# GpSimd takes the cosine products of the rotary embedding, VectorE copies both heads' transposed probabilities

## The chip, the cores and the metric

The kernel runs on one core of one Trainium2 chip. The metric is the device time of one execution in microseconds. A core has a matrix engine (TensorE, PE in the rows; its weight loads are PEld), a vector engine (VectorE, DVE), an activation engine (ScalarE, ACT), a general engine (GpSimd, POOL) and DMA queues; each engine runs its own list of instructions in order, and they meet only at semaphores. Matrix products land in PSUM, everything else lies in SBUF.

## The reference

Two transformer layers over 8 sequences of 128 tokens with 128 channels, in fp32. Layer 0 has a self-attention and a cross-attention (16 heads of 64 channels each) and an MLP; queries and keys are turned by a rotary embedding. Layer 1 has the same three parts with heads of 8 channels. Cut to what matters here (layer 0):

```python
def _rope(x, sin, cos):                 # on q and on k
    xe, xo = x[..., ::2], x[..., 1::2]
    re = xe * cos - xo * sin
    ro = xe * sin + xo * cos
    return jnp.stack((re, ro), axis=-1).reshape(x.shape)

def _attn(xq, ctx, wq, wkv, wo, bo):
    q = _heads(xq @ wq)
    k, v = jnp.split(ctx @ wkv, 2, axis=-1)
    q, k, v = _rope(q, sq, cq), _rope(_heads(k), sk, ck), _heads(v)
    sim = jnp.einsum('bhnd,bhmd->bhnm', q, k) * DH ** (-0.5)
    a = jax.nn.softmax(sim, axis=-1)
    return merge(jnp.einsum('bhnm,bhmd->bhnd', a, v)) @ wo + bo

x = _attn(adaln(x), adaln(x), ...) + x
x = _attn(adaln(x), ln(context), ...) + x
x = gelu(adaln2(x) @ w1 + b1) @ w2 + b2 + x
```

## The kernel before

Layer 0's attention is cut into 32 items (`ITEMS`): self- or cross-attention, times two halves of the batch (four sequences each), times eight pairs of heads. An item's tiles are 128 x 512 fp32: 128 channels of a pair of heads, by four sequences of 128 tokens. The work is a software pipeline written out by hand: each engine has a function `l0_slot(s)`, called for s = -2 to 31, and in slot s it handles stages of several items. There is no planner; the order within each engine's slot is the order of its code.

The stages of an item m, and who does them:

- `fill(m, f)` on PE: the query projection (f = 0) into PSUM bank X, the key projection (f = 1) into bank Y, the values (f = 2) into bank T[1]. In slot s these are for item s + 2.
- `evacuate_raw(m, f)` on ACT copies X or Y into the SBUF tile `raw` (for item s + 2); `evacuate_v` copies the values.
- `swap(m)`, two DMAs for each f on SP's queue, writes `raw` with neighbouring channels exchanged into `swp`.
- `rope_sine(m, f)` on GpSimd multiplies `swp` by the sines in place (item s + 1, L241). It waits first for the scores of slot s (`scores[0]`).
- `rope_cosine(m, f)` on VectorE multiplies the projection, read from the PSUM bank, by the cosines into `qk` (L652): for the keys of item s + 1, and the queries of item s + 2.
- `rope_sum(m, f)` on VectorE adds `swp` to `qk` (item s + 1, L658).
- `score(s)` on PE, `row_max(s, hh)` on VectorE (L635, from PSUM), `exp0(s, hh)` on ACT (L374), `normalise(s, hh)` on VectorE (a small reciprocal, then L642: both operands, `prob` and `rz`, lie in SBUF), for each of two heads hh.
- `transpose_probs(s, hh)` on PE (L908) into PSUM banks T[0] and T[1]; the copies to `probT` are VectorE's for head 0 (L648) and ACT's for head 1 (L380), in slot s + 1; then `prob_values` and `project_out` on PE.

PE's slot in order: score(s), transposes of (s-1, head 1), fill(s+2, 0), project_out(s-2), background, fill(s+2, 2), fill(s+2, 1), transposes of (s, head 0), prob_values(s-1). "Background" is the work of layer norms, context projections (slots 7 to 12), residuals and the MLP, set into single slots. A fill into X or Y waits until the bank has been read: by `rope_cosine`, which itself waits for `evacuate_raw`. In slot 26 GpSimd also computes a layer norm's inverse deviations, `inv_std(0, 2)` (L223), which VectorE's `ln_normalise` (L581) in the same slot waits for. Layer 1 begins behind slot 31, with `l1_slot(0)` taking the last probabilities of layer 0.

Of the kernel before, what the change touches and what calls it, by code (L numbers as in the profile page):

```python
# [58 lines left out]
def build(nc, small_in, x_in, ctx_in, ctxT_in, wqkv_in, wo_in, wmod_in, wsq_in, wff_in, row_in, out):  # L59
    es = ExitStack()  # L60
    with es:
# [157 lines left out]
        @block.gpsimd  # L219
        def _(pool):  # L220
            def inv_std(half, k):
                pool.wait_ge(ln_mv[half], k + 1)
                nc.gpsimd.tensor_tensor(rstd[:, half, :], vare[:, half, :], neg_half[:, 0:HALF], ALU.pow).then_inc(  # L223
                    ln_rstd[half], 1)

            def normalise_first(half, k):

                pool.wait_ge(ln_rstd[half], k + 1)
                for u in range(2):
                    last = nc.gpsimd.tensor_scalar(xn[:, HALF * half + u, :], x[:, HALF * half + u, :], mv[:, half, u, 0:1],  # L230
                                                   rstd[:, half, u:u + 1], ALU.subtract, ALU.mult)
                last.then_inc(ln_xn[half], 1)

            def context_inv_std(half):
                pool.wait_ge(ctx_mv, half + 1)
                nc.gpsimd.tensor_tensor(rstd_c[:, batches(half)], vare_c[:, batches(half)], neg_half[:, 0:HALF],
                                        ALU.pow).then_inc(ctx_rstd, 1)

            def rope_sine(m, f):
                pool.wait_ge(swapped[f][m % 2], 32 * (m // 2 + 1))  # L240
                nc.gpsimd.tensor_tensor(four(swp[:, m % 2, f, :]), four(swp[:, m % 2, f, :]), sin[f], ALU.mult).then_inc(  # L241
                    rope_sin[f], 1)

            def split_rows():
                pool.wait_ge(ld_rows, 16)
                src, done = rows, 0
                for j in range(3):
                    nc.gpsimd.tensor_copy(parts[:, j, :], src[:, :]).then_inc(row_part, 1)
                    done += 1
                    pool.wait_ge(row_part, done)  # L250
                    if j < 2:
                        nc.gpsimd.tensor_tensor(rest[:, :], src[:, :], parts[:, j, :], ALU.subtract).then_inc(row_part, 1)
                        done += 1
                        pool.wait_ge(row_part, done)
                        src = rest

            def mask_keys(a, half, j):

                pool.wait_ge(proj_out, AT["ck" if a else "k", half] + 1)
                if a:  # L260
                    for hh in range(2):
                        pool.wait_ge(scores1[hh], RUN * half + 2 * j + 2)
                ins = nc.gpsimd.tensor_scalar(km[:, half, j, :], k1[:, a, half, :], small[:, MASK + j:MASK + j + 1], None,
                                              ALU.mult)
                ins.then_inc(km_rest[half] if j else km_first[half], 1)

            def stage_values(half):
                pool.wait_ge(pv1, RUN * half + RUN)
                src = cv[:, half, :].rearrange("p (n h d) -> p n h d", h=2, d=DH1)
                for hh in range(2):  # L270
                    ins = nc.gpsimd.tensor_copy(value_slots(half, hh), src[:, :, hh, :])
                ins.then_inc(vst_out[half], 1)

            def l0_slot(s):
                if s in (2, 4):
                    context_inv_std(s // 2 - 1)
                if s in (12, 20):
                    inv_std(s // RUN - 1, 1)
                if 0 <= s < ITEMS - 1:
                    pool.wait_ge(scores[0], s + 1)  # L280
                if s + 1 < ITEMS:
                    rope_sine(s + 1, 0)
                    rope_sine(s + 1, 1)
                if s in (26, 30):
                    inv_std(0, 2 if s == 26 else 3)

            pool.dma_start(rows[:, :], row_in).then_inc(ld_rows, 16)
            inv_std(0, 0)
            inv_std(1, 0)
            split_rows()  # L290
            pool.memset(vst[:, :, :], 0.0).then_inc(padded, 1)
            pool.wait_ge(padded, 1)
            lanes = vst[:, :, :].rearrange("p a (n w) -> p (a n) w", w=2 * VW)
            pool.memset(lanes[:, :, DH1:DH1 + 49:48], 1.0).then_inc(padded, 1)
            pool.wait_ge(ld_tab, 16)
            for s in range(-1, ITEMS):
                l0_slot(s)
            for j in range(1, SLOTS):
                mask_keys(0, 0, j)
            inv_std(1, 2)  # L300
            normalise_first(1, 2)
            inv_std(1, 3)
            normalise_first(1, 3)
            for j in range(1, SLOTS):
                mask_keys(0, 1, j)
            for half in range(2):
                for j in range(SLOTS):
                    mask_keys(1, half, j)
                stage_values(half)
                inv_std(half, 4)  # L310
                normalise_first(half, 4)
            for half in range(2):
                inv_std(half, 5)
                normalise_first(half, 5)

        @block.scalar
        def _(act):
# [43 lines left out]
            def evacuate_raw(m, f):  # L361
                act.wait_ge(filled[f], m + 1)
                if m >= 2:
                    act.wait_ge(swapped[f][m % 2], 32 * (m // 2))
                nc.scalar.activation(raw[:, m % 2, f, :], (X, Y)[f][:, :], ACT.Copy).then_inc(raw_out[f], 1)  # L365

            def evacuate_v(m):
# [2 lines left out]

            def exp0(s, hh):
                act.wait_ge(rowmax[hh], s + 1)
                for u in range(HALF):
                    last = nc.scalar.activation(prob[:, hh, bcols(u)], S[hh][:, bcols(u)], ACT.Exp,  # L374
                                                bias=nmax[:, s % 2, hh, u:u + 1], accum_out=zsum[:, s % 2, hh, u:u + 1])
                last.then_inc(exps[hh], 1)

            def copy_T0(s):
                act.wait_ge(probs_T[1], s + 1)
                nc.scalar.activation(probT[:, s % 2, 1, :], T[1][:, :], ACT.Copy).then_inc(copied[1], 1)  # L380

            def evacuate_o(s):
                act.wait_ge(pv, s + 1)
# [39 lines left out]
            def l0_slot(s):  # L423
                loads(s)
                if s >= 2:
                    evacuate_o(s - 2)
                if s >= 1:
                    copy_T0(s - 1)
                if s >= 0:
                    exp0(s, 0)  # L430
                if s + 2 < ITEMS:
# [55 lines left out]
            def l1_slot(s):  # L487
                if s == 0:
                    evacuate_o(ITEMS - 2)
                    copy_T0(ITEMS - 1)  # L490
                if s == RUN:
                    copy_T1(s - 1)
                    evacuate_proj("q", 1)
# [56 lines left out]
        def _(dve):  # L550
# [92 lines left out]
                                        rz[:, s % 2, hh, :].unsqueeze(2).broadcast_to([P, HALF, P]), ALU.mult).then_inc(  # L643
                    norms[hh], 1)

            def copy_T0(s):
                dve.wait_ge(probs_T[0], s + 1)
                nc.vector.tensor_copy(probT[:, s % 2, 0, :], T[0][:, :]).then_inc(copied[0], 1)  # L648

            def rope_cosine(m, f):  # L650
                dve.wait_ge(raw_out[f], m + 1)
                nc.vector.tensor_tensor(four(qk[:, m % 2, f, :]), four((X, Y)[f][:, :]), cos[f], ALU.mult).then_inc(  # L652
                    rope_cos[f], 1)

            def rope_sum(m, f):
                dve.wait_ge(rope_sin[f], m + 1)
# [4 lines left out]
            def l0_slot(s):  # L661
                if s >= 1:
                    normalise(s - 1, 1)
                if s >= 0:
                    row_max(s, 0)
                    row_max(s, 1)
                if 0 <= s + 1 < ITEMS:
                    rope_cosine(s + 1, 1)
                if s in (26, 30):
                    ln_aggregate(2 if s == 26 else 3, 0)  # L670
                if s >= 1:
                    copy_T0(s - 1)
                if 0 <= s + 1 < ITEMS:
                    rope_sum(s + 1, 0)
                if s >= 0:
                    normalise(s, 0)
                if 0 <= s + 1 < ITEMS:
                    rope_sum(s + 1, 1)
                if s + 2 < ITEMS:
                    rope_cosine(s + 2, 0)  # L680
                background0(s)

            def background0(s):
# [57 lines left out]
            def l1_slot(s):  # L741
# [8 lines left out]
                    row_max1(s, 0)  # L750
                    row_max1(s, 1)
                if s == 0:
                    copy_T0(ITEMS - 1)
                middle1(s)
                if 1 <= s <= ITEMS and not first:
                    copy_T1(s - 1)
# [51 lines left out]
            ln_stats(0, 1)  # L808
            ln_aggregate(0, 1)
            dve.wait_ge(ld_tab, 16)  # L810
            l0_slot(-2)
            silu_condition()
            nc.vector.tensor_scalar(bq_scaled[:, :], vcol("b_q"), DH1 ** -0.5, None, ALU.mult)
            ln_normalise(0, 1)
# [7 lines left out]
        def _(pe):  # L822
# [33 lines left out]
            def fill(m, f):  # L856
# [8 lines left out]
                weights = wqkv[:, a * RUN + n, :]  # L865
                if f == 0:
                    if m:
                        pe.wait_ge(rope_cos[0], m)
                    if m == 31:
                        pe.wait_ge(gelu_done, 3)  # L870
                    mm(X[:, :], weights[:, 0:P], hT[:, half, :], True, True).then_inc(filled[0], 1)
                elif f == 1:
                    if m:
                        pe.wait_ge(rope_cos[1], m)
                    mm(Y[:, :], weights[0:width, P:2 * P], kv[:, half, :], True, True).then_inc(filled[1], 1)
                else:
                    if m:
# [120 lines left out]
            def l0_slot(s):  # L998
# [14 lines left out]
                    fill(s + 2, 1)  # L1013
                if s == 31:
                    project("q", 0)
                    pe.wait_ge(rope_cos[1], ITEMS)
                    project("k", 0)
                    project_values(0)
                transpose_probs(s, 0)
# [2 lines left out]
                if s == 28:  # L1022
# [1 line left out]
                    up(0, 0, 0, S[0])  # L1024
                    pe.wait_ge(exps[1], 29)
                    up(0, 0, 1, S[1])
                    pe.wait_ge(rope_cos[0], 31)
                    up(0, 0, 2, X)
                    pe.wait_ge(gelu_done, 1)
                    up(0, 0, 3, S[0])  # L1030
                if s == 30:
                    pe.wait_ge(rope_cos[0], ITEMS)
                    transpose_norm(3, 0, [X, X])

            def background0(s):
# [254 lines left out]
```

## Time and profile before

| what | value |
|---|---|
| median of three runs | 438.99 us (434.75 to 439.44) |
| the profiled execution | 439.93 us |
| its span | 437.9 us |
| TensorE clock granted in it, mean | 0.969 of full speed |
| PE / DVE / ACT / POOL busy | 89% / 73% / 70% / 31% |
| layer 0, first to last score | 22.28 to 267.26 us |

The span is the stretch from the first to the last instruction in the profile; the execution's time has 2.03 us more around it. Busy shares are averages over both layers; the argument needs single slots.

### The profile page before, as it was taken

To read this page: it belongs to the slowest core of one execution; us is meant where nothing else is said; L and a number is where in the kernel's file an instruction comes from. 1 tells how busy PE (TensorE), PEld (TensorE's weight loads), DVE (VectorE), ACT (ScalarE), POOL (GpSimd) and SP (SyncE) were. 2 spreads that over 40 slices of the span, in tenths; PEclk is the share of its full clock that TensorE was granted. 3 is DMA by queue.
4 is the path that set the end of the run, shared out by engine and by line. 5 is a ranking of instruction groups with operands and counts; after the bars stand their busy time and mean duration, and the time that the engine had idled before them with its cause. 6 is when DMAs were issued, how large, how long until landed. Compare 5 with 4: busy or idle time off the path is not lost.

```text
span 437.9 us, 9911 instructions
## 1 busy us (share of the span) xinstructions
PE 391.6 (89%) x3600; PEld 292.8 (67%) x3600; DVE 318.4 (73%) x685; ACT 307.1 (70%) x1052; POOL 136.6 (31%) x120
## 2 busy tenths in 40 slices
PE   7678999999989999989988988989898898898976
PEld 3355677777768777667666566867576687687654
DVE  4799898988878899978997575664557557557430
ACT  2277687877877786777768856697698678668722
POOL 1834433324333334324253230420473402002020
PEclk9899999999999999999999998999999979869999
DMA  5434424232441212121211010000000000000000
GB/s 171 149 111 126 162 91 157 72 121 77 132 159 48 99 71 75 57 77 61 85 61 62 36 49 1 2 2 0 1 1 2 1 1 2 1 2 1 1 24 24
DMA packets 17075, 26.08 MB, mean 60 GB/s; under 512 B 3615, under 2 KB 7973, under 8 KB 16901
## 3 DMA queue, kind: packets, MB, share of 16 engines
q1 hardware_dynamic: 13572, 18.43, 11.9%
q10 hardware_dynamic: 3424, 7.03, 5.3%
q8 instruction: 29, 0.48, 0.5%
q14 instruction: 18, 0.14, 0.1%
q0 software_dynamic: 32, 0.00, 0.0%
HBM read 8.15 MB, written 0.52 MB: 20 GB/s over the span
## 4 chain that ended last, share of the span: by engine, by line
PE 57%; DVE 23%; ACT 8%; issue 6%; POOL 2%; DMA 1%; POOLq 0%; SPq 0%; DVEq 0%; ACTq 0%
PE bank L824 44%; PE bank L1084 6%; PE bank L908 5%; DVE qk L658 4%; ACT prob L374 3%; DVE qk L652 3%; DVE nmax L720 3%; DVE prob L642 3%; DVE nmax L635 3%; DVE probT L648 2%; DVE xn L581 2%; ACT raw L467 1%; ACT hT L357 1%; PE bank L835 1%; DMA swp<-raw 1%
## 5 line engine op out<-in xcount | busy, mean ns | idle before, releaser
L241 POOL TENSOR_TENSOR swp<-swp,small 128x512 f32<-128x512 f32 x64 | 82.9, 1305 | 142.8 <-PE bank L824 115.4
L374 ACT ACTIVATE prob<-bank,nmax 128x128 f32<-128x128 f32 x256 | 91.2, 389 | 1.3 <-DVE nmax L635 1.3
L467 ACT ACTIVATE raw<-bank,nmax 128x128 f32<-128x128 f32 x256 | 73.4, 386 | 22.8 <-DVE nmax L720 22.8
L635 DVE TENSOR_REDUCE nmax<-bank 128x4 f32<-128x512 f32 x64 | 41.2, 685 | 29.1 <-PE bank L824 28.8
L720 DVE TENSOR_REDUCE nmax<-bank 128x4 f32<-128x512 f32 x64 | 41.2, 685 | 28.6 <-PE bank L824 28.5
L374 ACT ACTIVATION_READ_ACCUMULATOR prob<-bank,nmax 128x1 f32 x256 | 59.1, 231 | 0.0
L658 DVE TENSOR_TENSOR qk<-qk,swp 128x512 f32<-128x512 f32 x64 | 51.3, 803 | 5.0 <-POOL swp L241 5.0
L824 PE MATMUL bank<-hT,wqkv 128*128 128x512 f32 x96 | 49.8, 603 | 5.1 <-DVE qk L652 4.1
L908 PEld LDWEIGHTS bank<-small,prob 128*128 128x128 f32 x256 | 27.8, 140 | 39.0 <-DVE prob L642 29.0
L908 PE MATMUL bank<-small,prob 128*128 128x128 f32 x256 | 41.3, 284 | 13.6 <-DVE prob L642 13.3
L642 DVE TENSOR_TENSOR prob<-prob,rz 128x512 f32<-128x512 f32 x64 | 50.1, 782 | 2.2
L824 PE MATMUL bank<-km,q 32*128 32x128 f32 x512 | 39.6, 295 | 10.7 <-ACT raw L467 6.0
L223 POOL TENSOR_TENSOR rstd<-vare,neg_half 128x4 f32<-128x4 f32 x12 | 12.3, 1023 | 113.9 <-DVE vare L573 113.8
L652 DVE TENSOR_TENSOR qk<-bank,small 128x512 f32<-128x512 f32 x64 | 46.3, 723 | 0.7 <-ACT raw L365 0.7
L824 PEld LDWEIGHTS bank<-km,q 32*128 32x128 f32 x512 | 33.4, 197 | 18.0 <-issue 8.0
L380 ACT ACTIVATE probT<-bank 128x512 f32<-128x512 f32 x32 | 19.1, 597 | 37.2 <-PE bank L908 37.1
L365 ACT ACTIVATE raw<-bank 128x512 f32<-128x512 f32 x64 | 40.6, 636 | 1.9 <-PE bank L824 1.8
L824 PEld LDWEIGHTS bank<-wo,oT 128*128 128x128 f32 x256 | 33.0, 191 | 12.7 <-issue 12.1
L824 PE MATMUL bank<-probT,v 128*64 128x128 f32 x512 | 35.8, 283 | 4.0 <-ACT hT L357 3.2
L824 PE MATMUL bank<-qk 64*128 64x128 f32 x512 | 37.5, 286 | 2.0 <-DVE qk L658 1.0
L1084 PE MATMUL bank<-small,raw 128*128 128x128 f32 x256 | 38.4, 297 | 0.1
L824 PEld LDWEIGHTS bank<-qk 64*128 64x128 f32 x512 | 31.5, 189 | 8.4 <-issue 7.7
(106 smaller groups left out, 631.8 us busy)
## 6 DMA issues: line engine op xcount, KB each, us to landing
swp<-raw SPq DMA_DIRECT2D x128, 128.0 KB, 2.0
wqkv<-in_wqkv ACTq DMA_DIRECT2D x15, 192.0 KB, 2.5
wo<-in_wo ACTq DMA_DIRECT2D x2, 512.0 KB, 4.0
wff<-in_wff ACTq DMA_DIRECT2D x1, 1024.0 KB, 5.7
wsq<-in_wsq ACTq DMA_DIRECT2D x1, 576.0 KB, 4.6
x<-in_x SPq DMA_DIRECT2D x2, 256.0 KB, 4.2
wmod<-in_wmod ACTq DMA_DIRECT2D x1, 512.0 KB, 5.1
out_x<-x SPq DMA_DIRECT2D x2, 256.0 KB, 2.3
```

Of the source, the lines that this page charges most:

```text
L241: nc.gpsimd.tensor_tensor(four(swp[:, m % 2, f, :]), four(swp[:, m % 2, f, :]), sin[f], ALU.mult).then_inc(rope_sin[f], 1)
L365: nc.scalar.activation(raw[:, m % 2, f, :], (X, Y)[f][:, :], ACT.Copy).then_inc(raw_out[f], 1)
L374: last = nc.scalar.activation(prob[:, hh, bcols(u)], S[hh][:, bcols(u)], ACT.Exp, bias=nmax[:, s % 2, hh, u:u + 1], accum_out=zsum[:, s % ...
L467: last = nc.scalar.activation(prob1[:, s % 2, hh, bcols(u)], SB[(2 * s + hh) % 3][:, bcols(u)], ACT.Exp, bias=nmax[:, s % 2, hh, u:u + 1])
L635: nc.vector.tensor_reduce(nmax[:, s % 2, hh, :], four(S[hh][:, :]), AX.X, ALU.max, negate=True).then_inc(rowmax[hh], 1)
L642: nc.vector.tensor_tensor(four(prob[:, hh, :]), four(prob[:, hh, :]), rz[:, s % 2, hh, :].unsqueeze(2).broadcast_to([P, HALF, P]), ALU.mul ...
L652: nc.vector.tensor_tensor(four(qk[:, m % 2, f, :]), four((X, Y)[f][:, :]), cos[f], ALU.mult).then_inc(rope_cos[f], 1)
L658: nc.vector.tensor_tensor(qk[:, m % 2, f, :], qk[:, m % 2, f, :], swp[:, m % 2, f, :], ALU.add).then_inc(roped[f], 1)
L720: nc.vector.tensor_reduce(nmax[:, s % 2, hh, :], four(SB[(2 * s + hh) % 3][:, :]), AX.X, ALU.max, negate=True).then_inc(rowmax1[hh], 1)
L824: return nc.tensor.matmul(o, lhsT, rhs, start=start, stop=stop, skip_group_check=True)
L908: last = nc.tensor.transpose(T[hh][:, bcols(u)], prob[:, hh, bcols(u)], ident)
L1084: last = nc.tensor.transpose(T[hh][:, bcols(u)], prob1[:, s % 2, hh, bcols(u)], ident)
```

## The change

GpSimd takes over both cosine products of every item. It reads them from the SBUF copy `raw`, not from the PSUM banks. They stand last in its slot: after the two sines of item s + 1 come the two cosines of item s + 2. Its slot now waits for both heads' scores. The banks X and Y are free once `evacuate_raw` is done, so PE's fills wait for `raw_out` in place of `rope_cos`. VectorE loses its cosines, and gets the copy of head 1's transposed probabilities, ahead of head 0's; its two sums move together behind `normalise(s, 0)`. ACT loses that copy; its exponentials now wait for the transposes of the item before.

```diff
@@ gpsimd
+            def rope_cosine(m, f):
+                pool.wait_ge(raw_out[f], m + 1)
+                nc.gpsimd.tensor_tensor(four(qk[:, m % 2, f, :]), four(raw[:, m % 2, f, :]), cos[f], ALU.mult).then_inc(
+                    rope_cos[f], 1)
@@ gpsimd l0_slot(s), now from s = -2
                 if 0 <= s < ITEMS - 1:
                     pool.wait_ge(scores[0], s + 1)
-                if s + 1 < ITEMS:
+                    pool.wait_ge(scores[1], s + 1)
+                if 0 <= s + 1 < ITEMS:
                     rope_sine(s + 1, 0)
                     rope_sine(s + 1, 1)
+                if s + 2 < ITEMS:
+                    rope_cosine(s + 2, 0)
+                    rope_cosine(s + 2, 1)
                 if s in (26, 30):
                     inv_std(0, 2 if s == 26 else 3)
@@ scalar: evacuate_raw(m, f), m >= 2
                     act.wait_ge(swapped[f][m % 2], 32 * (m // 2))
+                    act.wait_ge(rope_cos[f], m - 1)
@@ scalar: exp0(s, hh)
+                if s:
+                    act.wait_ge(probs_T[hh], s)
@@ scalar: copy_T0 and its calls in l0_slot and l1_slot(0) are gone
@@ vector: rope_cosine and its calls are gone
-            def copy_T0(s):
+            def copy_T0(s, hh):
@@ vector l0_slot(s)
                     row_max(s, 0)
                     row_max(s, 1)
-                if 0 <= s + 1 < ITEMS:
-                    rope_cosine(s + 1, 1)
                 if s in (26, 30):
                     ln_aggregate(2 if s == 26 else 3, 0)
                 if s >= 1:
-                    copy_T0(s - 1)
-                if 0 <= s + 1 < ITEMS:
-                    rope_sum(s + 1, 0)
+                    copy_T0(s - 1, 1)
+                    copy_T0(s - 1, 0)
                 if s >= 0:
                     normalise(s, 0)
-                if 0 <= s + 1 < ITEMS:
+                if s + 1 < ITEMS:
+                    rope_sum(s + 1, 0)
                     rope_sum(s + 1, 1)
-                if s + 2 < ITEMS:
-                    rope_cosine(s + 2, 0)
@@ vector l1_slot(0)
-                    copy_T0(ITEMS - 1)
+                    copy_T0(ITEMS - 1, 0)
+                    copy_T0(ITEMS - 1, 1)
@@ tensor: fills of X and Y, and the other users of these banks
-                        pe.wait_ge(rope_cos[0], m)
+                        pe.wait_ge(raw_out[0], m)
```

## Rows read from the trace of the kernel before

**Rows 1.** The page: busy times, and the chain that ended last by engine.

```profile
PE 391.6 (89%) x3600; PEld 292.8 (67%) x3600; DVE 318.4 (73%) x685; ACT 307.1 (70%) x1052; POOL 136.6 (31%) x120
PE 57%; DVE 23%; ACT 8%; issue 6%; POOL 2%; DMA 1%; POOLq 0%; SPq 0%; DVEq 0%; ACTq 0%
```

**Rows 2.** Timeline of PE, scores of single slots: start, us, what.

```profile
137.40 1.16 PE L824 MATMUL bank<-qk 64*128 64x128 f32 x16
...
157.86 1.16 PE L824 MATMUL bank<-qk 64*128 64x128 f32 x16
165.05 1.16 PE L824 MATMUL bank<-qk 64*128 64x128 f32 x16
172.51 1.16 PE L824 MATMUL bank<-qk 64*128 64x128 f32 x16
```

**Rows 3.** Groups of 100 to 200 us, by form: busy us, mean ns | idle before.

```profile
L241 POOL TENSOR_TENSOR swp<-swp,small 128x512 f32<-128x512 f32 x27 | 34.1, 1275 | 58.1 <-PE bank L824 45.9 <-DMA swp<-raw 11.9
L658 DVE TENSOR_TENSOR qk<-qk,swp 128x512 f32<-128x512 f32 x27 | 20.3, 750 | 1.2 <-POOL swp L241 1.2
L652 DVE TENSOR_TENSOR qk<-bank,small 128x512 f32<-128x512 f32 x27 | 18.4, 681 | 0.0
L648 DVE COPY probT<-bank 128x512 f32<-128x512 f32 x14 | 9.5, 679 | 0.0
L380 ACT ACTIVATE probT<-bank 128x512 f32<-128x512 f32 x13 | 7.8, 597 | 14.6 <-PE bank L908 14.6
```

**Rows 4.** Timeline of slot 17, from the end of its scores.

```profile
152.16 1.29 DVE L635 TENSOR_REDUCE nmax<-bank 128x4 f32<-128x512 f32 x2 [0.84 <-PE bank L824]
152.21 2.62 POOL L241 TENSOR_TENSOR swp<-swp,small 128x512 f32<-128x512 f32 x2 [4.27 <-PE bank L824]
...
154.62 0.62 ACT L365 ACTIVATE raw<-bank 128x512 f32<-128x512 f32 x1
...
155.50 0.69 DVE L642 TENSOR_TENSOR prob<-prob,rz 128x512 f32<-128x512 f32 x1
...
156.94 0.67 ACT L365 ACTIVATE raw<-bank 128x512 f32<-128x512 f32 x1
```

**Rows 5.** Timelines of DVE and POOL where they overlap, slots 9 and 26.

```profile
93.12 0.68 DVE L658 TENSOR_TENSOR qk<-qk,swp 128x512 f32<-128x512 f32 x1
93.25 1.68 POOL L241 TENSOR_TENSOR swp<-swp,small 128x512 f32<-128x512 f32 x1 [1.22 <-DMA swp<-raw]
...
218.77 2.94 POOL L241 TENSOR_TENSOR swp<-swp,small 128x512 f32<-128x512 f32 x2 [4.27 <-PE bank L824]
218.81 1.76 DVE L642 TENSOR_TENSOR prob<-prob,rz 128x512 f32<-128x512 f32 x1
```

**Rows 6.** Timelines of POOL and PE, start of layer 0.

```profile
14.73 3.51 POOL L291 MEMSET vst<- 128x4096 f32 x1
...
18.49 2.49 POOL L241 TENSOR_TENSOR swp<-swp,small 128x512 f32<-128x512 f32 x2
...
22.28 1.16 PE L824 MATMUL bank<-qk 64*128 64x128 f32 x16 [0.51 <-DVE qk L658]
...
36.84 1.16 PE L824 MATMUL bank<-qk 64*128 64x128 f32 x16
```

**Rows 7.** The waits of layer 0, 22 to 275 us: total, times, longest.

```profile
POOL swp L241 <- DMA swp<-raw: 27.1, 16, 5.4
```

**Rows 8.** Timeline of slot 26: inverse deviations and the normalisation that waits for them.

```profile
222.94 1.01 POOL L223 TENSOR_TENSOR rstd<-vare,neg_half 128x4 f32<-128x4 f32 x1 [1.24 <-DVE vare L573]
...
225.99 1.11 DVE L581 TENSOR_SCALAR xn<-x,mv,rstd 128x128 f32<-128x128 f32 x4
```

**Rows 9.** Timeline of slot 0 of layer 1.

```profile
277.16 0.68 DVE L648 COPY probT<-bank 128x512 f32<-128x512 f32 x1
...
277.89 1.09 PE L824 MATMUL bank<-probT,v 128*64 128x128 f32 x16 [0.46 <-DVE probT L648]
```

**Rows 10.** The chain that ended last, in slot 13: start, us, what.

```profile
122.53 0.05 ACT probT L380
```

More of the change, by code:

```diff
@@ L295, in _ @@
             pool.wait_ge(ld_tab, 16)
-            for s in range(-1, ITEMS):
+            for s in range(-2, ITEMS):
                 l0_slot(s)
@@ L376, in exp0 @@
                 last.then_inc(exps[hh], 1)
-            def copy_T0(s):
-                act.wait_ge(probs_T[1], s + 1)
-                nc.scalar.activation(probT[:, s % 2, 1, :], T[1][:, :], ACT.Copy).then_inc(copied[1], 1)
             def evacuate_o(s):
@@ L426, in l0_slot @@
                     evacuate_o(s - 2)
-                if s >= 1:
-                    copy_T0(s - 1)
                 if s >= 0:
@@ L644, in normalise @@
                     norms[hh], 1)
[L646 to L653, printed above, removed]
+            def copy_T0(s, hh):
+                dve.wait_ge(probs_T[hh], s + 1)
+                nc.vector.tensor_copy(probT[:, s % 2, hh, :], T[hh][:, :]).then_inc(copied[hh], 1)
             def rope_sum(m, f):
@@ L671, in l0_slot @@
                 if s >= 1:
-                    copy_T0(s - 1)
-                if 0 <= s + 1 < ITEMS:
-                    rope_sum(s + 1, 0)
+                    copy_T0(s - 1, 1)
+                    copy_T0(s - 1, 0)
                 if s >= 0:
                     normalise(s, 0)
-                if 0 <= s + 1 < ITEMS:
+                if s + 1 < ITEMS:
+                    rope_sum(s + 1, 0)
                     rope_sum(s + 1, 1)
-                if s + 2 < ITEMS:
-                    rope_cosine(s + 2, 0)
                 background0(s)
@@ L752, in l1_slot @@
                 if s == 0:
-                    copy_T0(ITEMS - 1)
+                    copy_T0(ITEMS - 1, 0)
+                    copy_T0(ITEMS - 1, 1)
                 middle1(s)
@@ L810, in _ @@
             dve.wait_ge(ld_tab, 16)
-            l0_slot(-2)
             silu_condition()
@@ L873, in fill @@
                     if m:
-                        pe.wait_ge(rope_cos[1], m)
+                        pe.wait_ge(raw_out[1], m)
                     mm(Y[:, :], weights[0:width, P:2 * P], kv[:, half, :], True, True).then_inc(filled[1], 1)
@@ L1015, in l0_slot @@
                     project("q", 0)
-                    pe.wait_ge(rope_cos[1], ITEMS)
+                    pe.wait_ge(raw_out[1], ITEMS)
                     project("k", 0)
@@ L1026, in l0_slot @@
                     up(0, 0, 1, S[1])
-                    pe.wait_ge(rope_cos[0], 31)
+                    pe.wait_ge(raw_out[0], 31)
                     up(0, 0, 2, X)
@@ L1031, in l0_slot @@
                 if s == 30:
-                    pe.wait_ge(rope_cos[0], ITEMS)
+                    pe.wait_ge(raw_out[0], ITEMS)
                     transpose_norm(3, 0, [X, X])
```

## Prediction

> **What bounds the kernel now.** I read the page first [rows 1]: PE is busy 89% of the span, and 57% of the chain that ended last runs on it, 23% on VectorE and 8% on ACT. So PE is near its floor, and the rest of the chain shows that in some slots something else ends last. Only layer 0 is touched. Next the starts of the scores [rows 2]. The three slots 15 to 17 take 20.46 us together, 6.8 each; the chain there is PE alone, and slots 23 and 25 look the same. That is PE's floor for a slot without background: nothing done to VectorE or ACT shortens it. Slot 19 takes 7.46, and there VectorE is in the chain. Slots 7 to 12, with a projection more on PE, take about 7.6 and are PE's again. What the change can win lies only in slots like 19, some ten of them, each 0.4 to 0.9 us over its floor.
>
> Then who touches whose time. The two sines of a slot stand straight behind the scores [rows 4], while VectorE does its two row maxima, its cosine and its copy, which have one SBUF operand at most. Their durations don't move when GpSimd runs: 681 and 679 ns on average [rows 3] against 0.68 alone. The sums and the products `prob`·`rz` have two SBUF operands, and they do move [rows 5]. At 218.81 such a product, 0.69 us long otherwise, takes 1.76 and ends 0.53 us behind the end of the first of the two sines (218.77 + 1.27 = 220.04). At 93.25 a sine takes 1.68 in place of 1.27, as VectorE's sum had begun at 93.12. So these operations exclude each other. The two sines at 218.77 take 2.94 together in place of 2.49: a waiting VectorE operation gets in between two of GpSimd's. Before, this happens about once in two slots.
>
> **What the change does to a slot.** *VectorE* loses two cosines and gets one copy, which issue 0.60 us apart: 0.6 us less of some 6.0. *ACT* loses a copy of 0.60 [rows 3]. *GpSimd* gets two products of 1.25 to 1.27 us of the sines' kind and size: its row is the nearest there is, and I take 1.25, as for two sines in 2.49 [rows 6]; if the cosines were cheaper, the bound below would be that of VectorE's cosine, 0.68. Its slot goes from 2.5 to 5.0 us. *PE*'s fills lose the wait for the cosines, which isn't in the chain except at the start. The added wait on ACT for `probs_T` is over when the row maximum arrives (transposes stand before the exponentials anyway), and the one for `rope_cos` is two slots old: nothing.
>
> Where the cosines fall is the point. I lay one slot out, with 0 at the start of VectorE's row maxima (152.16 in [rows 4]). VectorE: maxima 0 to 1.2, copies to 2.4, reciprocal, product of head 0 at 2.6. ACT's exponentials start 0.73 behind and no longer wait for a copy, so `raw` of the queries is out at about 2.7 (it was 3.1: 154.62 + 0.62 - 152.16) and of the keys at 5.1 (it was 5.45). GpSimd: sines until 2.5, the first cosine wants to start at 2.8, is held by the product until 3.2, and runs to 4.45. It holds the first sum, which ends at 5.0; the second ends at 5.6. The second cosine wants 5.15, gets 5.45, runs to 6.7. It holds the product of head 1, ready at 5.7, which ends at 7.3. The next row maxima come behind that, at 7.2, and PE's transposes of head 1, which would be ready at 6.9, wait too. So a slot takes 7.2 us, whether VectorE has up to 1 us of background or none, as background now hides behind the held product.
>
> The Trainium skill (SBUF — State Buffer, Who interferes with whom) has the rule for this: GpSimd shares a port pair with VectorE, a VectorE operation with two SBUF inputs contends with a GpSimd one that reads SBUF, and whoever starts first has it for the whole instruction. The trace agrees, except that the hold is some 0.14 us shorter than the instruction (1.68 - 1.27 = 0.41 from 93.25, while the sum ended at 93.80). By whole instructions a slot would need 4 x 1.27 + 4 x 0.68 = 7.8 us; with the hand-over of the rows the eight need about 6.8 to 7.1, and the layout above gives 7.2.
>
> **The sum**, in us against the profiled 439.93:
> - Slots 15, 16, 17, 23, 25: 6.8 to 7.2, +2.0.
> - Slots 3 to 5, 18 to 20, 22 and 24, with VectorE in the chain now, 7.2 to 7.7: they come to 7.2 to 7.4. Worth -1.8 together, of which slot 25's overrun into 26 (the 1.76 us product) is -0.7.
> - Slots 7 to 12: PE's floor of 7.6 is above 7.2: 0.
> - Slots 2, 6, 13, 21, 27, where ACT's copy stands in the chain [rows 10]: exponentials start 0.35 earlier, -1.7.
> - Late swaps. GpSimd waited 16 times for a swap, 27.1 us in all, the longest 5.4 [rows 7]; ten or so of these sines came 0.8 to 2.4 us late within a full slot. `raw` is now out 0.65 to 0.95 us earlier relative to the next slot, which heals about half. For the others everything behind the sine, two cosines more, is late, and the second cosine can pass the second sum, which costs the scores 1.2 us. I take four slots of 0.3: +1.2, bounds 0 and ten slots of 1.2, +12.
> - The start of layer 0. Before, GpSimd is busy until 18.49 (a memset of 3.51), then does two sines, and the first scores come at 22.28 [rows 6]. Now two cosines stand ahead of the sines: +2.5, less some 0.5 as PE has its fills behind it already: first scores at 24.3. The cosines of item 1 come before its sines too, on a GpSimd that has no gap: my layout gives 31.8 and 39.2 for the next two scores, against 28.46 and 36.84 [rows 6]. +2.4.
> - Slot 26. `inv_std(0, 2)` ran at 222.94 and VectorE normalised at 225.99 [rows 8]. It now stands behind two cosines, the last of which waits for the keys' `raw`: it ends some 7.9 us behind the row maxima at 220.5, so the normalisation starts at 228.5 in place of 226.0, and head 1's product and the next slot's maxima are queued behind it on VectorE. +2.5.
> - The seam to layer 1: PE's last `prob_values` of layer 0 wait for VectorE's copy [rows 9]; one copy more is +0.6. ACT's lost copy gives nothing back there, since its second exponentials wait behind that PE step.
>
> Total: 2.0 - 1.8 - 1.7 + 1.2 + 2.4 + 2.5 + 0.6 = +5.2, so the profiled execution would take 445. The profiled one was 0.9 above the median, so against the median 438.99 I say 444.5 (rounded up from 444.2).
>
> **Rivals.**
> 1. *The order at the port goes wrong in many slots.* In the layout the second cosine arrives 0.25 us behind the start of the second sum. Where it arrives ahead of it, the sum ends at 6.7, the scores end at 7.9, and a slot is 8.0, not 7.2. For: any late sine does this. Against: both times hang on the same row maxima. In twelve more slots, +0.8 each: 454.
> 2. *Losses and gains cancel.* The slots settle at 6.9 rather than 7.2 since GpSimd's share of a held operation is shorter than I have read it from two rows, and the start costs 1 rather than 2.4, as later slots had slack for it: 5.2 - 1.5 - 1.4 = +2.3 or less, less another 1 from the slots with VectorE in the chain: 440.5.
> 3. *Faster: VectorE's relief reaches PE's floor.* The place is slots 2 to 6, 18 to 20, 22 and 24, whose excess over PE's floor is 2.3 + 3.6 us. If the cosines fall into the 2.4 us of VectorE's maxima and copies, or delay only what has slack, this excess goes, with ACT's 1.7: -7.6, against 3 left of the start, slot 26 and the seam. 434.3. It decides from the point at which GpSimd's second cosine is through before the second product is ready; for that `raw` of the keys must be out 1 us earlier, and ACT's list in [rows 4] says no.
>
> That the change does not do what it says leaves no rival: the waits are replaced one for one.
>
> The Trainium skill warns in the same sense (Perfetto Trace Analysis, Optimizing Scalar/DVE Operations): as both engines share a read port, moving work between them might not help. The rows of this case decide, since it depends on where the operations fall.
>
> **Chances.** Forecast 0.52, rival 1 0.15, rival 2 0.20, rival 3 0.13. No change that can be told is within 1%, 434.6 to 443.4. The forecast's own range is 441 to 448; it lies above 443.4 for about two thirds. So faster 0.10, same 0.38, slower 0.52. The range leaves out half of rival 3 and the upper half of rival 1: 436 to 454.
>
> **What would show it.** Busy time of GpSimd in layer 0 up by 64 x 1.27 = 81 us; the mean of VectorE's sums (750 ns) and products up to 0.9 to 1.2 us, that of row maxima and copies unchanged; slots 15 to 17 at 7.2, with VectorE or GpSimd in their chain; first scores at 24.3; the normalisation of slot 26 2.5 us later. If slots 15 to 17 stay at 6.8, the layout is wrong; if they are at 8.0, rival 1 holds.

## The result, and the profile after

The changed kernel takes 465.73 us (median of 5; 464.46 to 475.7) against 436.26 (median of 5): 1.067 times as long, 95% interval 1.061 to 1.073. In two later runs the same kernel gave 1.080 (1.075 to 1.086) and 1.056 (1.047 to 1.065). The direction was right and the size far off: +29.5 us, where +5.5 was forecast and 454 was the end of the range. The first profile of the changed kernel fell in a slow execution (475.7 us), so rows and lengths of slots are taken from a later one of the same kernel (`e15_again`, 464.1 us, span 462.0).

The page of the changed kernel, for [rows 1]: GpSimd works 96 us more, while ACT works 14 less and VectorE is busy 26.5 us longer although its work got less. Being held counts as busy.

```profile
PE 395.3 (86%) x3600; PEld 298.5 (65%) x3600; DVE 344.9 (75%) x653; ACT 293.1 (63%) x1020; POOL 232.6 (50%) x184
PE 47%; DVE 35%; issue 6%; ACT 5%; DMA 1%; POOL 1%; POOLq 0%; SPq 0%; DVEq 0%
```

The groups of 100 to 200 us, for [rows 3]: sums went from 750 to 1220 ns and products from 762 to 924, row maxima and copies did not move. A cosine takes 1539 ns where a sine took 1275, as it is itself held.

```profile
L246 POOL TENSOR_TENSOR qk<-raw,small 128x512 f32<-128x512 f32 x25 | 38.5, 1539 | 17.7 <-ACT raw L375 17.5
L241 POOL TENSOR_TENSOR swp<-swp,small 128x512 f32<-128x512 f32 x26 | 33.2, 1294 | 8.3 <-PE bank L820 5.0 <-DMA swp<-raw 3.4
L658 DVE TENSOR_TENSOR qk<-qk,swp 128x512 f32<-128x512 f32 x24 | 28.4, 1220 | 0.0
L647 DVE TENSOR_TENSOR prob<-prob,rz 128x512 f32<-128x512 f32 x26 | 24.0, 924 | 0.9
L640 DVE TENSOR_REDUCE nmax<-bank 128x4 f32<-128x512 f32 x26 | 16.7, 681 | 2.8 <-PE bank L820 2.6
L653 DVE COPY probT<-bank 128x512 f32<-128x512 f32 x26 | 16.6, 678 | 0.0
```

A steady slot (16) of the changed kernel, for [rows 4]: from row maxima at 158.94 to row maxima at 166.12, 7.18 us; its neighbours take 7.18 and 7.16. The pair of sums takes 2.37 in place of 1.3, the first of them being held by the first cosine, and the product of head 1 takes 1.56 in place of 0.69 and ends 0.55 us behind the second cosine.

```profile
158.91 2.50 POOL L241 TENSOR_TENSOR swp<-swp,small 128x512 f32<-128x512 f32 x2 [0.43 <-PE bank L820]
158.94 1.27 DVE L640 TENSOR_REDUCE nmax<-bank 128x4 f32<-128x512 f32 x2
...
161.53 0.69 DVE L647 TENSOR_TENSOR prob<-prob,rz 128x512 f32<-128x512 f32 x1
161.73 1.63 POOL L246 TENSOR_TENSOR qk<-raw,small 128x512 f32<-128x512 f32 x1 [0.33 <-ACT raw L375]
162.14 2.37 DVE L658 TENSOR_TENSOR qk<-qk,swp 128x512 f32<-128x512 f32 x2
164.10 1.54 POOL L246 TENSOR_TENSOR qk<-raw,small 128x512 f32<-128x512 f32 x1 [0.74 <-ACT raw L375]
...
164.63 1.56 DVE L647 TENSOR_TENSOR prob<-prob,rz 128x512 f32<-128x512 f32 x1
...
166.12 1.27 DVE L640 TENSOR_REDUCE nmax<-bank 128x4 f32<-128x512 f32 x2
```

The start, for [rows 6]: first scores at 25.79, not at 22.28.

```profile
14.75 3.51 POOL L300 MEMSET vst<- 128x4096 f32 x1
...
18.50 2.49 POOL L246 TENSOR_TENSOR qk<-raw,small 128x512 f32<-128x512 f32 x2
20.94 2.49 POOL L241 TENSOR_TENSOR swp<-swp,small 128x512 f32<-128x512 f32 x2
22.24 3.40 DVE L658 TENSOR_TENSOR qk<-qk,swp 128x512 f32<-128x512 f32 x2 [7.82 <-POOL swp L241]
23.38 3.38 POOL L246 TENSOR_TENSOR qk<-raw,small 128x512 f32<-128x512 f32 x2
25.79 2.08 PE L820 MATMUL bank<-qk 64*128 64x128 f32 x16 [9.22 <-DVE qk L658]
```

Slot 26, for [rows 8], is where the forecast's list has a hole. The inverse deviations come late, as forecast. But the four normalisations behind them then take 3.01 us in place of 1.11: they fall on the sines of the next slot and end 0.59 behind those (246.39 + 2.48 = 248.87).

```profile
245.41 1.01 POOL L223 TENSOR_TENSOR rstd<-vare,neg_half 128x4 f32<-128x4 f32 x1
246.39 2.48 POOL L241 TENSOR_TENSOR swp<-swp,small 128x512 f32<-128x512 f32 x2
246.45 3.01 DVE L586 TENSOR_SCALAR xn<-x,mv,rstd 128x128 f32<-128x128 f32 x4 [2.14 <-POOL rstd L223]
```

Where the time went, in us, by starts of row maxima: `e15_again` (span 462.0) against before (437.9). The last column is the difference in another execution of the same kernel, `e0_again` (span 468.8):

| stretch | before | e15_again | difference | in e0_again |
|---|---|---|---|---|
| up to the first maxima | 23.4 | 27.9 | +4.4 | +4.5 |
| slots 4, 5, 12, 20, 26 (VectorE normalises) | 7.06, 7.70, 7.77, 7.71, 7.39 | 8.48, 9.20, 10.03, 9.22, 11.68 | +11.0 | +16.5 |
| slots 15 to 17 and 23 | 6.76, 6.81, 6.89, 6.76 | 7.18, 7.18, 7.16, 7.16 | +1.5 | +1.5 |
| slots 1, 3, 7, 22, 24 | 7.74, 7.67, 7.69, 7.70, 7.62 | 8.54, 9.47, 9.17, 8.25, 8.98 | +6.0 | +3.6 |
| the other 17 slots | | | +0.2 | +4.4 |
| behind the maxima of slot 31 | 169.1 | 170.0 | +0.9 | +0.4 |

So the late start, the normalisation slots and the steady slots lose in both executions, while the size of the loss in the other slots changes from one to the other.

### The profile page after: what moved, and what is told of

It reads as the page before. It is cut to its first block, busy times and chain, and to the rows that moved or that the text cites. A ratio compares the mean times of both kernels' runs of the same rounds, so it can differ in the third digit from the quotient of the medians.

```text
span 473.6 us, 9973 instructions
## 1 busy us (share of the span) xinstructions
PE 406.5 (86%) x3600; PEld 306.0 (65%) x3600; DVE 344.1 (73%) x653; ACT 294.5 (62%) x1020; POOL 233.6 (49%) x184
## 4 chain that ended last, share of the span: by engine, by line
PE 49%; DVE 30%; issue 5%; ACT 5%; DMA 4%; POOL 1%; SPq 0%; POOLq 0%; DVEq 0%
PE bank L820 37%; DVE qk L658 9%; PE bank L1080 6%; DVE prob L647 4%; DVE nmax L640 4%; DMA swp<-raw 4%; DVE probT L653 4%; PE bank L904 3%; DVE nmax L716 3%; DVE xn L586 2%; ACT raw L473 1%; ACT prob L386 1%; PE bank L831 1%; DVE x L566 1%; POOL swp L241 1%
## 5 line engine op out<-in xcount | busy, mean ns | idle before, releaser
L246 POOL TENSOR_TENSOR qk<-raw,small 128x512 f32<-128x512 f32 x64 | 97.8, 1532 | 53.5 <-ACT raw L375 53.4
L658 DVE TENSOR_TENSOR qk<-qk,swp 128x512 f32<-128x512 f32 x64 | 78.9, 1268 | 12.3 <-POOL swp L241 12.3
L647 DVE TENSOR_TENSOR prob<-prob,rz 128x512 f32<-128x512 f32 x64 | 58.2, 909 | 2.2
L904 PEld LDWEIGHTS bank<-small,prob 128*128 128x128 f32 x256 | 30.3, 145 | 44.0 <-DVE prob L647 25.8
L386 ACT ACTIVATION_READ_ACCUMULATOR prob<-bank,nmax 128x1 f32 x256 | 56.2, 219 | 0.0
L820 PE MATMUL bank<-hT,wqkv 128*128 128x512 f32 x96 | 54.6, 655 | 1.3 <-ACT hT L366 1.0
L820 PEld LDWEIGHTS bank<-qk 64*128 64x128 f32 x512 | 33.4, 196 | 27.9 <-issue 26.7
L820 PEld LDWEIGHTS bank<-wo,oT 128*128 128x128 f32 x256 | 36.6, 209 | 14.6 <-issue 14.4
L653 DVE COPY probT<-bank 128x512 f32<-128x512 f32 x64 | 40.9, 679 | 0.0
L820 PE MATMUL bank<-wo,oT 128*128 128x128 f32 x256 | 37.5, 294 | 0.0
```

The costliest lines, as they stand in the source:

```text
L246: nc.gpsimd.tensor_tensor(four(qk[:, m % 2, f, :]), four(raw[:, m % 2, f, :]), cos[f], ALU.mult).then_inc(rope_cos[f], 1)
L647: nc.vector.tensor_tensor(four(prob[:, hh, :]), four(prob[:, hh, :]), rz[:, s % 2, hh, :].unsqueeze(2).broadcast_to([P, HALF, P]), ALU.mul ...
L653: nc.vector.tensor_copy(probT[:, s % 2, hh, :], T[hh][:, :]).then_inc(copied[hh], 1)
L658: nc.vector.tensor_tensor(qk[:, m % 2, f, :], qk[:, m % 2, f, :], swp[:, m % 2, f, :], ALU.add).then_inc(roped[f], 1)
L820: return nc.tensor.matmul(o, lhsT, rhs, start=start, stop=stop, skip_group_check=True)
L904: last = nc.tensor.transpose(T[hh][:, bcols(u)], prob[:, hh, bcols(u)], ident)
```

## The experiments

A ratio is that to the kernel before, measured beside it, with its 95% interval.

**e0_again.** The changed kernel, unchanged.

> The changed kernel once more, unchanged, for a profile at the time that most of its executions take: 465 us. If the clock explains a large part of the loss, TensorE's granted clock is below 0.9 in single stretches of layer 0, right behind gaps of 3 us and more on PE; in the first profile these were 20 to 30 us (0.52) and 70 to 80 us (0.66).

470.1 us, 1.080 (1.075 to 1.086). The clock was 0.54 from 20 to 30 us and 0.76 from 68 to 82 us.

**e1_copy_back** and **e2_copies_only** take the change apart.

```diff
# e1, from the changed kernel: head 1's copy on ACT again
+ act: if s >= 1: copy_T0(s - 1)          # ahead of exp0(s, 0)
- dve: copy_T0(s - 1, 1)
# e2, from the kernel before: cosines stay on VectorE
- act: copy_T0(s - 1)
+ dve: copy_T0(s - 1, 1)                  # ahead of copy_T0(s - 1, 0)
```

> The changed kernel with the copy of head 1 on ACT again; the cosines stay on GpSimd. If the cosines' hold on VectorE is the cause: 458 to 465 us, slots 15 to 17 at 6.8 to 7.1 in place of 7.2, since VectorE's own list gets 0.6 shorter but its sums and normalisations still wait for GpSimd. If the second copy on VectorE is the cause: near 440 us.

> The kernel before with both copies on VectorE and nothing else; cosines stay on VectorE. If the cosines on GpSimd are the cause of the loss: 438 to 444 us, as VectorE gets 0.6 us a slot more in the ten slots where it is in the chain. If the copy is the cause: near 460 us.

e1: 473.3 us, 1.088 (1.082 to 1.095). Giving the copy back does not help at all: slots 15 to 17 take 7.5 to 7.65, where 6.8 to 7.1 was expected. In its steady slot VectorE, with a copy less, stands idle for ACT, whose exponentials again start behind the copy:

```profile
169.62 0.18 DVE L652 RECIPROCAL rz<-zsum 128x4 f32<-128x4 f32 x1 [0.98 <-ACT prob L386]
169.84 0.69 DVE L654 TENSOR_TENSOR prob<-prob,rz 128x512 f32<-128x512 f32 x1
```

So with the cosines on GpSimd the copy is better off on VectorE. e2: 448.5 us, 1.027 (1.018 to 1.035). Its slots 15 to 19 all take 7.35 us, VectorE's list, but its profiled execution was only 4 us over before's (span 442.0 against 437.9); the other 8 us of the median I can't place. The copies alone do cost, yet less than half of the whole. In the steady slots the cosines do not add to it: in the changed kernel slots 15 to 17 take 7.17.

**e3_writes_only.** GpSimd's cosines become writes that read nothing; the queries and keys lose their cosine part.

```diff
-nc.gpsimd.tensor_tensor(four(qk[..., f, :]), four(raw[..., f, :]), cos[f], ALU.mult)
+nc.gpsimd.memset(scratch[:, :], 0.0)      # 128 x 1024
+nc.gpsimd.memset(qk[:, m % 2, f, :], 0.01)
```

> The changed kernel with each cosine product replaced by two memsets on GpSimd of 1.3 us together (by 3.51 us for 4096 elements in the start), which read nothing: the queries and keys lose their cosine part, everything else runs. If VectorE's two-operand sums and products are held by GpSimd's reads only: sums fall to some 0.8 us and slots 15 to 17 to 6.8, and the time to 445 to 452, with the four-fold normalisations of slots 4, 5, 12, 20 and 26 still slow (2 to 3 us in place of 1), since before the change a memset held one. If GpSimd's longer list alone is the cause (its sines come later): 460 or more, with sums at 0.7.

447.7 us, 1.031 (1.022 to 1.040): 22 us less than e0_again beside it, with GpSimd at work almost as long (busy 226 us against 231). Slots 15 to 17 take 6.65, 7.00 and 6.68. Slot 12 fell to 7.55, against the expectation. But slots 4, 5, 20 and 26 still take 9.5, 9.0, 8.5 and 11.7. Slot 20 shows a normalisation at 2.00 us beside memsets alone:

```profile
182.39 2.00 DVE L590 TENSOR_SCALAR xn<-x,mv,rstd 128x128 f32<-128x128 f32 x4
182.75 0.95 POOL L250 MEMSET scratch<- 128x1024 f32 x1 [0.68 <-ACT raw L379]
183.64 0.66 POOL L251 MEMSET qk<- 128x512 f32 x1
```

**e4_yield.** GpSimd lets VectorE's normalisations pass.

```diff
+if s in (26, 30): inv_std(...)                        # moved ahead of the cosines
 rope_cosine(s + 2, 0)
+if s in (4, 5): pool.wait_ge(ctx_n, s - 3)
+if s in (12, 20): pool.wait_ge(ln_xn[s // RUN - 1], 2)
+if s == 26: pool.wait_ge(ln_xn[0], 3)
 rope_cosine(s + 2, 1)
```

> The changed kernel, in which GpSimd waits in slots 4, 5, 12, 20 and 26 with its last cosine until VectorE's normalisation of that slot is through, and computes the inverse deviations of slot 26 ahead of its cosines. The normalisations read and write SBUF with one tensor operand and stood for 2 to 3 us in place of 1. If these collisions (and the low clock behind them) cost what the slots show, 13.5 us in the five: the ratio to the kernel before falls from 1.067 to 1.080 by 0.02 or more, with the normalisations at 1.0 us and slot 26 below 9. If GpSimd's cosines elsewhere make the whole loss, or the wait costs what it saves: ratio unchanged.

457.8 us, 1.055 (1.050 to 1.061). The fairest comparison is with the two variants of the changed kernel that ran beside it, e5 and e6 below: 1.079 and 1.073. The unchanged kernel gave 1.067, 1.080 and 1.056 in its own runs. In slot 26 the four normalisations are back at 1.10, ahead of the cosine that waits for them (each takes 333 to 336 ns):

```profile
245.94 1.10 DVE L592 TENSOR_SCALAR xn<-x,mv,rstd 128x128 f32<-128x128 f32 x4
246.96 0.16 DVE L651 RECIPROCAL rz<-zsum 128x4 f32<-128x4 f32 x1
247.12 1.27 POOL L246 TENSOR_TENSOR qk<-raw,small 128x512 f32<-128x512 f32 x1 [2.86 <-DVE xn L592]
247.16 1.78 DVE L653 TENSOR_TENSOR prob<-prob,rz 128x512 f32<-128x512 f32 x1
```

Slot 26 fell to 9.54, not below 9; the delayed cosine holds the product for 1.1 us (last line). The five slots with a normalisation take 43.9 us together: 37.6 before, 48.6 in e15_again, 46.2 in e3.

**e13_writes_and_yield.** Both remedies at once: e3's memsets and e4's waits.

> The changed kernel with the cosines replaced by memsets that read nothing (the queries and keys lose their cosine part), and GpSimd waiting for the five normalisations with the second of them. If the two kinds of hold at the port are the whole loss but for the late start: 438 to 443 us, slots 4, 5, 20 and 26 at 7.2 to 8.7 in place of 8.5 to 11.7. If 448 us stay, something else is slow in those slots.

437.3 us, 0.9985 (0.9935 to 1.0035): the kernel before's time, with both copies on VectorE, GpSimd's list as long and the start late. The first maxima still come 3.7 us later than before; the 31 slots behind them take 9.2 us less than before, so the equality is in part a sum of opposite terms. Slots 15 to 17 take 6.65, slots 4, 5, 12, 20 and 26 take 6.9, 7.3, 7.6, 6.9 and 7.7. In its slot 18 VectorE's product and sums stand at their full speed beside the memsets:

```profile
164.06 0.69 DVE L657 TENSOR_TENSOR prob<-prob,rz 128x512 f32<-128x512 f32 x1
164.24 0.95 POOL L250 MEMSET scratch<- 128x1024 f32 x1
164.67 1.28 DVE L668 TENSOR_TENSOR qk<-qk,swp 128x512 f32<-128x512 f32 x2
165.13 0.52 POOL L251 MEMSET qk<- 128x512 f32 x1
```

**e7_queries_back** and **e14_half_and_yield** do half of the change: `rope_cosine(s + 2, 0)` on VectorE behind the sums, from bank X, the keys' on GpSimd; e14 adds e4's waits and e8's memset (below).

> The changed kernel with the queries' cosine back on VectorE, read from PSUM behind the two sums; the keys' stays on GpSimd. By holds at the port: the sums go free (0.8 us on average in place of 1.25), slots 15 to 17 at 6.8 to 7.1, the ratio to the kernel before about half of the loss, 1.03 to 1.045. If GpSimd's own length is what counts and not what it holds: the loss follows VectorE's added 0.6 us a slot, ratio 1.07 or more.

> Keys' cosine alone on GpSimd (queries' back on VectorE), GpSimd yields to the five normalisations, and the memset stands behind slot 28. If the effects add up from 450.6 us: 440 to 444 us, slot 26 below 9.5. It is faster than the kernel before only if the holds that remain are all covered.

e7: 450.6 us, 1.039 (1.030 to 1.047), slots 15 to 17 at 6.9; its sums average 748 ns, where the changed kernel's take 1269 by the page. e14: 443.7, 1.016 (1.010 to 1.022), slot 26 at 9.1. Half of the cosines cost about half; what remains is still more than the relief of VectorE gives.

**e10_cosine_after_sum** has GpSimd's second cosine wait for `roped[1] >= s + 2` in every slot.

> The changed kernel, in which GpSimd's second cosine waits for VectorE's second sum of the slot, everywhere. Pairs of sums that took 3.4 us in place of 2.4, where a cosine got between them behind a late swap, are gone; there were four or so. If that order costs what rival 1 priced, 0.8 us each: 3 us less, ratio 0.007 lower. If the delayed cosine costs as much in the next slot: unchanged.

468.8 us, 1.077 (1.069 to 1.085), no change. Slots 15 to 17 rose to 7.4. Slots 1, 3, 7, 22 and 24 took 41.6 us together, against 44.4 in e15_again and 42.1 in e0_again, which is within what one kernel shows from one execution to the next. Since the remedy costs 0.2 us in every steady slot, it does not price the order by itself.

**e6_start_on_vector**: items 0 and 1 have their cosines on VectorE, ahead of its loop. **e11_all_mended**: e4, e6, e10 and the later memset in one.

> The changed kernel with the cosines of items 0 and 1 on VectorE, read from the same copies, ahead of the loop; GpSimd begins its own with item 2. If the late start is GpSimd's four products in a row behind its memset: first row maxima near 24 us in place of 28, and 3 to 5 us less in all. If the gap is closed by something else later (swaps, loads): less than 1 us.

> The changed kernel with every remedy at once: GpSimd yields to the five normalisations and to the second sum, items 0 and 1 have their cosines on VectorE, the memset stands behind slot 28. If the effects add up (13 for the normalisations, 4 for the start, 3 for the memset and the order): 446 to 452 us, ratio 1.02 to 1.035, and what is left is 0.4 us a slot at the port and a late swap here and there. If it comes to the kernel before, 436: the steady hold is free.

e6: 466.8 us, 1.073 (1.067 to 1.078); the first maxima are at 24.9 in place of 27.9, and the interval overlaps those of e5 (1.074 to 1.084) and of the unchanged kernel, so a gain of the whole is not shown. e11: 456.4, 1.049 (1.041 to 1.056): the effects did not add up, it is hardly better than e4 alone. Its first maxima come at 22.6, 5.2 us ahead of e15_again's, but its slots 1 to 7 take 7.9 to 9.8 and lose 3.5 of these again; why is open.

**The clock** was the rival that the profile brought up: e5 warms PE at the start, e12 and e16 (the same kernel) in five gaps, e15 is the unchanged kernel beside e16.

```diff
+if s == 0: keep_warm(28, S[0])                        # e5
+if s in (5, 6, 13, 21, 27):                           # e12, e16, behind score(s)
+    pe.wait_ge(raw_out[0], s + 2); keep_warm(14, X)
```

> The changed kernel with 28 more matrix products on PE, of zeros into a bank that is free, in the 9 us gap ahead of the first scores. If the clock that fell there to 0.52 of full speed matters: granted clock near 1.0 from 20 to 30 us, slot 0's PE work 1 to 2 us shorter, time 1 to 2 us less. If slot 0 is bound by GpSimd anyway: time unchanged within 1 us although the clock is up.

> The changed kernel with 14 matrix products of zeros on PE in each of slots 5, 6, 13, 21 and 27, in the gap in which it waits for the held product behind a normalisation. If the low clock behind these gaps costs time of its own: granted clock 1.0 there, and 3 to 6 us less. If PE's slow stretch is covered by the engine that it waits for next: the clock is up and the time unchanged.

> The changed kernel with 14 matrix products of zeros in each of the gaps of slots 5, 6, 13, 21 and 27, now beside the changed kernel on the same chip. If the low clock behind the gaps costs time of its own: 3 to 5 us less than the run beside it, with intervals apart. If not: within 1.5 us of it.

> The changed kernel unchanged, as the measure on the same chip for the run with warmed gaps: ratio to the kernel before 1.065 to 1.085.

e5: 469.7 us, 1.079 (1.074 to 1.084), no gain. But it only moved the low stretch: the granted clock fell at 24.75 in place of 18.85, and the first scores took 2.08 us as without warming, so it does not test what the clock costs. e12: 465.4 us, 1.069 (1.061 to 1.076), below e0_again's 1.080 on another chip. On one chip e16 gave 1.059 (1.054 to 1.064) and e15 1.056 (1.047 to 1.065), no difference. That ratio of e15, however, rests on two of its six executions, 459.8 and 464.1 us; the other four took 469 to 472. Over all six the medians are 469.6 for e15 and 463.4 for e16, all of whose executions lie between 461.3 and 466.0. So these runs do not settle what the low clock costs; a gain of 3 to 6 us is not excluded.

In e16 slot 27 got shorter than in e15 (7.87 against 8.99) and slots 12 and 26 longer (10.64 and 13.12 against 10.03 and 11.68).

Slot 26 of the unchanged kernel shows that the clock can cost time of its own. In e0_again it takes 14.63 us, in e15_again 11.68. In e0_again the granted clock was 0.5 from 244.3 to 251.1 us, just behind the maxima of this slot (243.08), so PE's fills came late and the keys' `raw` started 7.95 us behind the maxima, not 4.86; the second cosine, the inverse deviations and the normalisations are all queued behind it. First e15_again (maxima at 238.51), then e0_again:

```profile
241.40 1.07 PE L820 MATMUL bank<-wqkv,ctxnT 96*128 96x128 f32 x8
243.37 0.60 ACT L375 ACTIVATE raw<-bank 128x512 f32<-128x512 f32 x1 [0.26 <-PE bank L820]
...
247.37 1.91 PE L820 MATMUL bank<-wqkv,ctxnT 96*128 96x128 f32 x8
251.03 0.60 ACT L375 ACTIVATE raw<-bank 128x512 f32<-128x512 f32 x1 [1.11 <-PE bank L820]
```

The low clock stood behind a gap of 2.0 us on PE, in which it waited for a product on VectorE. So it is a consequence of the gaps and adds to what they cost; in the changed kernel its share of the whole stays open.

**e8_before_memset_later** is the kernel before, with the 3.5 us memset on GpSimd behind its sines of slot 28.

> The kernel before, with GpSimd's 3.5 us memset for layer 1 moved from the start to behind its sines of slot 28. If GpSimd's writes hold VectorE's one-operand normalisations, the four at the start go from 4.8 to 1.1 us, the first scores come 3 us earlier, and the time is 2 to 3.5 us less: a kernel faster than both. If the swaps of item 0 end last at the start anyway: no gain.

434.1 us, 0.994 (0.991 to 0.998): 1 to 4 us less than the kernel before, and so less than both kernels. The normalisations at the start take 1.48 in place of 4.77 us and the first scores come at 19.79 in place of 22.28:

```profile
13.16 1.48 DVE L582 TENSOR_SCALAR xn<-x,mv,rstd 128x128 f32<-128x128 f32 x4
...
19.79 1.16 PE L825 MATMUL bank<-qk 64*128 64x128 f32 x16 [2.48 <-DVE qk L659]
```

## Why the prediction was wrong

The direction and the main mechanism held. The layout of a steady slot gave 7.2; it measured 7.16 to 7.18 in slots 15 to 17 and 23 of all profiles of the changed kernel, with the same two holds. The five slots on PE's floor cost +1.8 (four at +0.4, slot 25 +0.3) for +2.0. e3 shows that the holds by the cosines' reads are most of the loss (22 of 34 us over the kernel before), and e13 that nothing of it is left when both kinds of hold are taken away. From profile to profile (span 462.0 against 437.9) the loss is 24 us, for which the sum had 5.2.

**The step that failed** is the statement of who is held: "So these operations exclude each other", drawn from two-operand operations alone, and with it "whether VectorE has up to 1 us of background or none, as background now hides behind the held product". Background that normalises does not hide: it reads and writes SBUF with one tensor operand, and GpSimd holds it too, whether GpSimd reads or only writes (e3's slot 20). Slots 4, 5, 12, 20 and 26 cost 11.0 us (16.5 in e0_again), for which the sum had 2.5 for slot 26 (lateness alone), nothing for slot 12 and a gain for 4, 5 and 20. With the reads gone but the writes there (e3) they still cost 8.6, slot 26's lateness included; when GpSimd also lets the normalisations pass and computes the inverse deviations first (e13) they cost nothing. In e0_again about 3 us of slot 26 are the clock's, as shown above. The trace of before had a line for it, which was not among the rows: at the start, beside GpSimd's 3.51 us memset [rows 6], which the prediction used only as GpSimd's occupation.

```profile
13.55 4.77 DVE L581 TENSOR_SCALAR xn<-x,mv,rstd 128x128 f32<-128x128 f32 x4
```

**The late start** was mis-sized. The first scores came 3.5 us later, where the layout had 2.0, and the third 5.0 us later, for its +2.4. The two sums took 3.40 us: the first is held by a sine, as it was before (1.74), but the second now too, by a cosine of item 1, which the layout did not have there. The scores themselves take 2.08 us in place of 1.16 on the low clock behind the gap, so the first maxima are 4.4 late; the sum had no term for the clock.

**The late swaps** were mis-sized, as far as the runs show it. Slots 1, 3, 7, 22 and 24 cost 6.0 in e15_again and 3.6 in e0_again, where +1.2 was taken (bounds 0 and 12). GpSimd's waits for swaps fell from 27.1 us [rows 7] to 13.3 in e15_again and 8.5 in e0_again, by half or more as forecast, but a late slot now has twice as much queued behind the sine. Rival 1's order does occur: in e15_again the second sum is held as well (1.75 us) in slots 1, 7, 22 and 24, so in four slots and not in twelve. In e0_again it is not held in slots 7 and 24, and these take 7.53 and 7.16 in place of 9.17 and 8.98. But e10, which changes the order, gained nothing. Whether the order or the late swap behind it costs the time stays open.

**The gains did not come.** The slots with VectorE in the chain were to give 1.8, and those with ACT's copy 1.7. Slots 2, 6, 13 and 21 gave 1.5 together, but 27 lost 0.6, 19 gave nothing, and 18, 22 and 24 lost. e2 shows the other side: the second copy takes VectorE's list to 7.35 where cosines stay.

**The seam** was put at +0.6; everything behind the maxima of slot 31 took 0.9 more in e15_again and 0.4 in e0_again.

The Trainium skill (SBUF — State Buffer, Who interferes with whom) covers the failed step: it counts `tensor_scalar` among the operations that can enter a mode that uses both ports, when their operands meet its conditions, and says that this mode contends with GpSimd, with no exception for GpSimd's writes. The measurements agree with it: 1.11 us alone against 3.01 beside two sines, and 4.77 beside a memset. No run here shows in which mode the normalisations ran. The prediction used only the section's part on two inputs.

## What to carry to other kernels

Before moving work to GpSimd, list every VectorE operation of the stretch with both operands in SBUF and every one that goes from SBUF to SBUF, with their waits; each was held here for the rest of a GpSimd product that it met, and busy shares (here 31%) don't show it. In this kernel GpSimd's products were free only beside the VectorE operations that read PSUM, the row maxima and copies. Long GpSimd writes that nobody needs yet (a memset for a later layer) belong in a stretch in which VectorE does not go from SBUF to SBUF.

## What the runs showed of the hardware

- Two GpSimd operations in a row let a waiting two-operand VectorE operation in between them (2.94 us for two sines, in [rows 5]). The four one-operand normalisations of slot 26 did not delay the two sines (2.48 us), but each sine held one of them: the first two took 1.28 and 1.30 us, the last two 0.33.
- GpSimd's memsets leave VectorE's two-operand operations alone (0.69 and 1.28 us in e13's rows), but hold its one-operand SBUF operations (4.77 us beside 3.51).
- TensorE's granted clock was 0.55 over 20 to 30 us in e15_again, behind 9 us of idle time on PE, that is mostly at its lower level of 1.2 GHz, at which the 16 products of the scores take 2.08 us in place of 1.16. With PE kept busy for 6.2 us of this gap (e5) the clock fell later (0.74 over the same stretch), but the scores still took 2.08.
- A low clock can make a slot longer although PE was waiting before it: 14.63 us in place of 11.68 in slot 26 (e0_again and e15_again).
